# The seams between four stages of one kernel: groups prepared early, nineteen steps of the fourth stage placed inside the third's end, and a changed load order

## The reference

```python
h = jnp.maximum(_layernorm(x, axis=-1), 0.0)
x = x + _L0_gnn_ref(h, adj, Wq, bq, Wk, bk, Wv, bv, Wo, bo)   # masked attention, 8 heads of 32
h = jnp.maximum(_layernorm(x, axis=-1), 0.0)
x = x + _L1_gnn_ref(h, adj, W, b)          # deg * (h Wi + b) + adj @ (h Wj)
h = jnp.maximum(_layernorm(x, axis=-1), 0.0)
x = x + _L2_gnn_ref(h, adj, W_heads, a_heads, W_out, a_out, w1, b1, w2, b2, gamma, beta)
                                           # 4 GAT heads, ELU, one more GAT layer, ELU, FFN, layernorm
h = jnp.maximum(_layernorm(x, axis=-1), 0.0)
x = x + _L3_gnn_ref(h, adj, W, a)          # one GAT head; concat([attention out, h W])
```

## Time and profile before

| What | us |
|---|---|
| median of three runs (lowest to highest) | 1535.41 (1535.36 to 1536.48) |
| the profiled execution | 1534.9 |
| its span, from first to last instruction | 1533.1 |
| busy: PE / DVE / ACT / POOL | 1393.3 / 1261.6 / 1020.0 / 363.4 |
| mean granted TensorE clock | 0.969 of 2.4 GHz |

### The profile page before, as it was taken

How to read it: one execution, slowest core, us unless ns; L and a number is a source line. 1 busy time by engine, 2 the same in 40 slices (tenths; PEclk the granted TensorE clock), 3 DMA queues, 4 the chain that set the end, 5 groups by cost and what they waited for, 6 DMA issues and landing times.

```text
span 1533.1 us, 36480 instructions
## 1 busy us (share of the span) xinstructions
PE 1393.3 (91%) x11709; PEld 1245.7 (81%) x11709; DVE 1261.6 (82%) x3014; ACT 1020.0 (67%) x3244; POOL 363.4 (24%) x683
## 2 busy tenths in 40 slices
PE   5999999999969996899999999999999999965776
PEld 4888888888859995788888988889889889954554
DVE  4788887767647775889999999999999999956887
ACT  3788888788745554776766766766767667624776
POOL 1222222222126662111221211212212111103332
PEclk8999999999969997999999999999999999986999
DMA  7500000000000000000000000000000000000112
GB/s 247 152 1 0 0 0 0 0 0 0 1 1 0 0 0 1 1 1 1 1 0 0 0 0 0 0 0 0 0 0 0 0 0 1 1 1 21 62 62 76
DMA packets 23894, 24.26 MB, mean 16 GB/s; under 512 B 1953, under 2 KB 23201, under 8 KB 23713
## 3 DMA queue, kind: packets, MB, share of 16 engines
q1 hardware_dynamic: 23120, 23.54, 4.8%
q10 hardware_dynamic: 720, 0.07, 0.0%
HBM read 15.21 MB, written 8.39 MB: 15 GB/s over the span
## 4 chain that ended last, share of the span: by engine, by line
PE 59%; ACT 17%; DVE 14%; issue 8%; POOL 1%; DVEq 1%; DMA 0%; ACTq 0%; SPq 0%; POOLq 0%
PE bank L1412 11%; ACT probs L938 11%; PE bank L1438 9%; PE bank L1425 7%; PE bank L1499 3%; PE bank L1218 3%; PE bank L1322 2%; PE bank L1313 2%; PE bank L1488 2%; PE bank L1354 2%; PE bank L1366 2%; PE bank L1368 2%; PE bank L1367 2%; PE bank L1399 2%; PE bank L1300 2%
## 5 line engine op out<-in xcount | busy, mean ns | idle before, releaser
L938 ACT ACTIVATE probs<-bank,negtop 128x128 f32<-128x128 f32 x512 | 185.2, 414 | 49.6 <-DVE negtop L665 49.6
L284 POOL TENSOR_TENSOR var_eps<-mv,eps_tile 128x2 f32<-128x2 f32 x128 | 48.1, 376 | 520.9 <-DVE mv L272 520.9
L300 ACT ACTIVATE h<-x_all,shift,rstd 128x256 f32 (+1 forms) x256 | 139.8, 597 | 40.0 <-POOL shift L290 40.0
L489 POOL TENSOR_TENSOR var_y<-mv_y,eps_tile 128x2 f32<-128x2 f32 x32 | 16.5, 516 | 570.6 <-DVE mv_y L806 570.6
L1438 PE MATMUL bank<-wout_hi,headsT_hi 128*128 128x258 f32 x512 | 151.0, 295 | 0.0
L1438 PE MATMUL bank<-wout_lo,headsT_hi 128*128 128x258 f32 x512 | 144.4, 282 | 0.0
L1438 PE MATMUL bank<-wout_hi,headsT_lo 128*128 128x258 f32 x512 | 144.3, 282 | 0.0
L1425 PE MATMUL bank<-probsT,whs 128*128 128x128 f32 x1024 | 136.2, 276 | 0.0
L938 ACT ACTIVATION_READ_ACCUMULATOR probs<-bank,negtop 128x1 f32 x512 | 129.7, 253 | 0.0
L1425 PEld LDWEIGHTS bank<-probsT,whs 128*128 128x128 f32 x1024 | 124.5, 192 | 0.5
L257 DVE BATCH_NORM_STATS2 st<-x_all 128x6 f32 (+1 forms) x256 | 95.1, 414 | 19.8 <-DMA x_all<-in_x 19.7
(11 more groups left out here) (232 smaller groups left out, 4631.6 us busy)
## 6 DMA issues: line engine op xcount, KB each, us to landing
x_all<-in_x SPq DMA_DIRECT2D x32, 256.0 KB, 2.8
out_x<-x_all SPq DMA_DIRECT2D x32, 256.0 KB, 2.1
wh<-in_L_gnn_W_heads SPq DMA_DIRECT2D x2, 512.0 KB, 8.1
a_heads<-in_L_gnn_a_heads SPq DMA_DIRECT2D x1, 1024.0 KB, 10.9
wout<-in_L_gnn_W_out SPq DMA_DIRECT2D x1, 1024.0 KB, 10.4
raw<-in_L_gnn_W SPq DMA_DIRECT2D x1, 512.0 KB, 6.1
ffn<-in_L_gnn_w SPq DMA_DIRECT2D x2, 256.0 KB, 6.1
probsT<-in_L_gnn_Wq SPq DMA_DIRECT2D x1, 256.0 KB, 3.6
```

Of the source, the lines that this page charges most:

```text
L284: nc.gpsimd.tensor_tensor(var_eps[:, p, :], mv[:, p, :, 1], eps_tile[:, :], ALU.add).then_inc(s.norm, 1)
L300: last = nc.scalar.activation(h[:, p, c, :], x_all[:, bass.ds(g * G + c, 1), :].rearrange("p a d -> p (a d)"), ACT.Relu, bias=shift[:, p, ...
L938: last = nc.scalar.activation(probs[:, r, i, :], bank[4 + r][:, i * N:(i + 1) * N], ACT.Exp, bias=negtop0[:, r, i:i + 1], scale=float(DH) ...
```

## The change

- **Start.** `x` groups 2 and 3 are issued before the late loads. The issue of group 3 waits until group 1 has landed. `LATE_FIRST` becomes 4 and `late_masks` moves from step 1 to step 3.
- **Seams between the first three stages.** Groups 0 and 1 of the second and third stage are prepared in steps 30 to 33 of the stage before, in the places where that stage would have prepared groups 32 and 33 (`pre_group`, `early`). The next stage starts at t = 0. The waits of the engines for the whole stage are gone, except one each on TensorE inside the next stage (step 1). The second stage's weights are transposed and split in step 32 of the first. The third stage's small weights are split in steps 1 to 3 of the second; `wh` is split in two halves in step 0 of the third, behind `hT2_hi` on ScalarE and behind `right` on VectorE, `wout` at the end of that step.
- **Third and fourth stage.** In each of the steps 33, 34 and 35 of the third stage, seven steps of the fourth (t = -2 to 18 in all) are called at seven places (`last_stage_step`). The fourth stage's own loop begins at t = 19. Its score tiles become `t4`, `p4T`, `sum4`, `negtop4` and `rsum4_c` in place of those that it shared with the third stage.

```diff
-def run_steps(eng, groups, step, turn=2, deepest=3):
-    first = (deepest + turn) // turn * turn
-    for t in range(-2, first):
+def run_steps(eng, groups, step, turn=2, deepest=3, begun=-2):
+    first = (max(deepest, begun - 1) + turn) // turn * turn
+    for t in range(begun, first):
         step(Step(t, t % turn, groups))
...
+PLACES = 7
+DRAINING = 3
+def last_stage_step(at, place, step):
+    i = at.t - at.groups - 1 if isinstance(at.t, int) else -1
+    if i >= 0:
+        t = i * PLACES + place - 2
+        step(Step(t, t % 4, at.groups))
+LAST_BEGUN = PLACES * DRAINING - 2
...
+        def early(k, g):
+            return k in (1, 2) and isinstance(g, int) and g < 2
+        def pre_group(k, at, lag):
+            there, g, p = at.group(lag)
+            if there:
+                return not early(k, g), k, g, p
+            return k < 2 and isinstance(g, int) and NG <= g < NG + 2, k + 1, g - NG if isinstance(g, int) else g, p
...
         def pre_dve(dve, k, at):
-            there, g, p = at.group(-2)
+            there, k, g, p = pre_group(k, at, -2)
...
+            if k == 3 or early(k, g):
+                dve.wait_ge(pre[k - 1].x, g + 1)
...
-        LATE_FIRST = 2
+        LATE_FIRST = 4
...
+            for p in range(2):
+                sp.wait_ge(x_loaded[p], 16)
+                sp.dma_start(x_group(2 + p), x_d[:, (2 + p) * G:(3 + p) * G, :]).then_inc(x_loaded[p], 16)
             for dst, src in LATER_LOADS:
                 sp.dma_start(dst, src).then_inc(later_loads_done, 16)
-            with sp.Fori(1, NG // 2) as i:
+            with sp.Fori(2, NG // 2) as i:
...
                 if b and isinstance(gb, int) and gb == NG - 1:      # PE, step0
+                    transpose_weights1()
...
             if PHASES > 1:                                          # PE
-                pe.wait_ge(pre[0].x, NG)
                 pe.wait_ge(weights_act, 5)
                 pe.wait_ge(w1_lo, 2)
-                run_steps(pe, NG, step1)
+                run_steps(pe, NG, step1, begun=0)
...
             def step2(at):                                          # DVE
...
                 if o2:
                     low_head(3, go)
+                last_stage_step(at, 0, step3)
...
+                    if not positive(g):
+                        for half in range(2):
+                            heads = slice(2 * half, 2 * half + 2)
+                            dve.wait_ge(w_hi, 4 + half)
+                            nc.vector.tensor_tensor(wh_lo[:, :, heads], wh[:, :, heads], wh_hi[:, :, heads].bitcast(FP32),
+                                                    ALU.subtract).then_inc(w_lo, 1)
                 if l:
                     dve.wait_ge(scores3, gl + 1)
...
+                last_stage_step(at, 1, step3)
...
+                last_stage_step(at, 6, step3)
                 if isinstance(at.t, int) and at.t == 0:
-                    dve.wait_ge(w_hi, 3)
+                    dve.wait_ge(w_hi, 6)
                     nc.vector.tensor_tensor(flat(wout_lo), flat(wout), flat(wout_hi).bitcast(FP32), ALU.subtract).then_inc(w_lo, 1)
...
-            if PHASES > 3:
-                dve.wait_ge(pre[2].x, NG)
-                run_steps(dve, NG, step3, 4)
+            run_steps(dve, NG, step2, deepest=4, begun=0)
+            run_steps(dve, NG, step3, 4, begun=LAST_BEGUN)
```

More of the change, by code:

```diff
@@ L293, in pre_act @@
         def pre_act(act, k, at, lag=-1):
-            there, g, p = at.group(lag)
+            there, k, g, p = pre_group(k, at, lag)
             if not there:
@@ L479, in step1 @@
                     pre_pool(pool, 1, at)
-                run_steps(pool, NG, step1)
+                run_steps(pool, NG, step1, begun=0)
             if PHASES > 2:
-                pool.wait_ge(pre[1].x, NG)
                 def step2(at):
                     there, g, p = at.group(4)
+                    for k in range(3):
+                        last_stage_step(at, k, step3)
                     if there:
@@ L671, in step0 @@
                         top(r)
+                if b and isinstance(gb, int) and gb == NG - 1:
+                    low_weights1()
                 if b:
@@ L705, in _ @@
             if PHASES > 1:
[L706 to L711, removed]
+                run_steps(dve, NG, step1, begun=0)
             def step2(at):
@@ L1067, in step2 @@
                     nc.scalar.copy(hT2_hi[:, :, :, :], bank[0][:, :].rearrange("p (k c n) -> p k c n", k=KC, c=G)).then_inc(hT2_high, 1)
+                    if not positive(g):
+                        act.wait_ge(o1_full, NG)
+                        for half in range(2):
+                            heads = slice(2 * half, 2 * half + 2)
+                            nc.scalar.copy(wh_hi[:, :, heads], wh[:, :, heads]).then_inc(w_hi, 1)
                 if m:
@@ L1146, in step2 @@
                     project_out(3)
+                if isinstance(at.t, int) and at.t == 0:
+                    nc.scalar.copy(flat(wout_hi), flat(wout)).then_inc(w_hi, 1)
                 if o2:
@@ L1226, in neighbours, with transpose_weights1 @@
                 return last
+            def transpose_weights1():
+                pe.wait_ge(later_loads_done, LATER_LOADED)
+                nc.tensor.transpose(bank[6][:, 0:N], adj_f[:, :], ident).then_inc(weights_T, 1)
+                for i in range(2):
+                    for k in range(KC):
+                        for c in range(KC):
+                            last = nc.tensor.transpose(bank[4 + i][:, (k * KC + c) * N:(k * KC + c + 1) * N],
+                                                       raw1[:, c, (i * KC + k) * N:(i * KC + k + 1) * N], ident)
+                    last.then_inc(weights_T, 1)
             def step0(at):
@@ L1409, in project @@
                             pe.wait_ge(whs_ready, g * 4 + 1 + half)
+                        if c == 0 and not positive(g):
+                            pe.wait_ge(w_lo, 4 + half)
                         for k in range(KC):
@@ L1592, in step3 @@
                     for c in range(G):
-                        last = nc.tensor.matmul(bank[4][:, c * F3:(c + 1) * F3], p3T[:, c, :], h3[:, at.quarter(2), c, 0:F3], start=True, stop=True)
+                        last = nc.tensor.matmul(bank[4][:, c * F3:(c + 1) * F3], p4T[:, c, :], h3[:, at.quarter(2), c, 0:F3], start=True, stop=True)
                     last.then_inc(at4_full, 1)
```

157 lines of the change are left out of this document (85 added, 72 removed).

## The result

The changed kernel took 1498.37 us (median of 4 runs, 1495.48 to 1499.15), the kernel before beside it 1535.38: a ratio of 0.9759, with a 95% interval of 0.9748 to 0.9771. That is 37.0 us less, where 43.8 were forecast (1491.6); the time lies within the forecast's 1484 to 1500. The profiled execution took 1499.15 us with a span of 1497.3; mean granted clock 0.98.

What follows compares the result with a forecast made beforehand. No engine was taken to bound the four places changed, only chains of engines waiting on each other; inside stages TensorE or VectorE is nearly always busy. 10.5 + 7.0 + 5.9 + 20.4 = 43.8 off 1534.9, plus 0.5: 1491.6 us (1484 to 1500, 60%).

Steps and rivals of the forecast that it cites:

- Start, 10.5: At the start, loading `x` group 2 ahead of the late loads gains 9.7 to 11.7 us, taken as 10.5.
- First to second stage, 7.0: At the first seam, TensorE goes on 7.5 us sooner, less 0.5 for extra splits: 7.0 us gained (5.5 to 7.5).
- The 0.5 for the extra splits in steps 1 to 3: In the second stage's filling steps, weight splits on ScalarE and VectorE cost 0.5 us, 2 at most.
- Second to third stage, 5.9: At the second seam, features start 7.1 us sooner, `wh` is hidden, `wout` gives back 1.2: 5.9 us gained.
- Drain and fourth stage, 20.4: Third stage's drain mixed with the fourth's start: the stretch falls from 125.4 to 105 us, gaining 20.4 (bounds 2 and 37.9).
- rival 1: The drain overlaps hardly at all: stretch of 123.5 us, a gain of 1.9, time 1510.1; chance 12%.
- rival 5: Every drain place synchronises all engines, so each step runs alone: 27.3 us more there, time 1539; chance 3%.
- rival 3: VectorE is the only bound, busy 95% in the mixed stretch: 92 us, a gain of 33, time 1479; chance 14%.
- so I count it at the upper level: In the mixed stretch, 82 us of TensorE work in 105 us is counted at the upper clock level, 2.4 GHz.
- the 13.3% and the quarter of 17.45: Mixed stretch: VectorE busy 17.33 of 20 us gives 101; a quarter of its 17.45 us drain idling, 4.4, gives 105.
- Rival 2: The clock stays low in the mixed stretch: 29.2 us more, a stretch of 134.2, time 1520.8; chance 5%.

Runs made afterwards that it cites:

- the second profile: The changed kernel itself, run again without any change, beside the kernel before: 1496.26 us, ratio 0.9754.
- seams_undone: Changed kernel with the first two groups of the second and third stage prepared in their own stage again, weights' places as changed: 1513.42 us, ratio 0.9864.
- wout_halves: Changed kernel with `wout` rounded and subtracted in two halves, ScalarE's halves put into its two waits in step 0 of the third stage: 1489.81 us, ratio 0.9714.
- tail_apart: Changed kernel, but the fourth stage starts only after the third has ended, with no places in steps 33 to 35: 1507.18 us, ratio 0.9830.
- ffn_after_place: Changed kernel with eight places per drain step in place of seven, the first FFN product one place later in steps 33 to 35: 1489.08 us, ratio 0.9698.
- seam_warm: Changed kernel with 12 spare TensorE products ahead of the features in step 1 of the third stage, `wout` in one piece: 1493.23 us, ratio 0.9732.
- x_behind_late: Changed kernel with the loads of `x` groups 2 and 3 issued behind the late loads again: 1508.02 us, ratio 0.9836.

## Why the prediction was right, and which step of it was not

- *Start, 10.5.* Right, 9.8. The chain that is late next was the one named; `h` of group 2 came at 23.30 where 22.8 was read off.
- *First to second stage, 7.0.* The mechanism was right, the size too small: 11.6. The hole of 445.18 - 437.20 = 7.98 went whole. Not priced was the work on either side of it, which had run at the lower level: the last output product gave 1.7 us, and the next three steps went from 15.26 us (445.18 to 460.44) to 13.51 (11.93 in the second profile). The 0.5 for the extra splits in steps 1 to 3 does not show. *seams_undone* brings back hole and slow fill together, but not the slow output product, which takes 1.99 to 2.00 us in every run with the moved weights.
- *Second to third stage, 5.9.* 4.4. The features came 7.8 us nearer the last `x` (7.1 forecast) and `wh` was hidden. But `wout` gave back 2.6 by the `hT_lo` of step 1 and not 1.2. The cover that failed is ScalarE's: the FFN's 1.13 us that went away counted for nothing, since ScalarE then stood waiting for TensorE (1.09 and 0.81 us) ahead of `wout`. *wout_halves* uses just these waits. That leaves 5.2, of which 4.4 reach step 33: from the `hT_lo` of step 2 on this took 717.6 us before, 718.6 in the first profile and 717.4 in the second, so the difference is scatter.
- *Drain and fourth stage, 20.4.* This is the step that failed, by half: 10.1. Order, work and place were right (*tail_apart* puts the overlap at 10 to 11 us, not the 1.9 of rival 1; rival 5's 27 us of loss and rival 3's 95% of VectorE are out, it was busy 75%). What failed is the sentence "so I count it at the upper level". The stretch ran at 0.90, and its 115.3 us lie just outside the 97 to 113 that the forecast allowed. With the same order held at 0.98 it took 109.1, so 6.2 of the 10.3 us between 105 and 115.3 are the clock's; the remaining 4 are more idle time of VectorE than the 13.3% and the quarter of 17.45 that were left for it. *ffn_after_place* gets as much by order, without spare products, so clock and uncovered hops are not two separate sums. Rival 2 had the mechanism and a price of 29.2 that was nearly five times too large, because TensorE does not stay low: the clock fell to 0.50 and 0.61 behind waits of 3.44 and 3.03 us and was 1.00 again some microseconds later.

That the sum came out only 8 us off the span's 35.8 is in part luck: it owes something to the first seam, whose 4.6 us of unforeseen gain made up for nearly half of the drain's loss.

By the Trainium skill (TensorE: Matmul & The Clock Gate, "Part 1: The HAM clock gate") throttled is the default and activity releases it. The traces here agree: the rows of the FFN product above have 0.41 and 0.28 for the same matmul, behind waits of 3.03 and 1.31 us. The prediction cited that rule and set it aside on the strength of the steady part's 1.00 at a busy share of 14.54 of 20 us; the mean share did not tell how the waits were spread.

One thing stays open. The changed kernel's two profiles have different clocks in step 33 (0.91 and 0.87, 38.69 and 39.55 us) for one and the same program, and *wout_halves* and *seam_warm*, whose drain is that program too, have 0.83 and 0.95 (41.15 and 37.04 us). What decides between them was not tried.

## What to carry to other kernels

When two stages are interleaved, cover a hop between engines on the engine that waits for it: here a TensorE that stood still for 3.03 us paid a second time, in matmuls that started every 0.21 us in place of 0.12. Price a seam not by its hole alone but with the slow work on either side. Work that is moved "beside" other work must be put into a wait that its own engine really has, on the near side of what holds that engine up.

## What was not expected of the hardware

- Spare products made the program faster: 12 in one wait brought the next step from 17.3 to 18.1 down to 16.3 us, and 100 in the drain (4 in each of 19 places, 24 ahead of the FFN) brought 115.3 to 109.1 us, though TensorE's busy time there rose from 76 to 87 us.
- The same code took from 114.2 to 118.3 us for the same stretch in six profiles, in the order of the granted clock: 114.2 (*seam_warm*) and 115.3 at 0.90, 115.4 (*seams_undone*) and 116.2 at 0.89, 116.6 (*x_behind_late*) at 0.87, 118.3 (*wout_halves*) at 0.86.
